# Self attention of the last stage: scores three pieces ahead, slots that begin with turns, and turns as ordinary matmuls with the identity

## The chip, the cores and the metric

The kernel runs on one core of one Trainium2 chip. The metric is device time in microseconds of one execution, and lower is better. TensorE is called PE below, VectorE DVE, ScalarE ACT, GpSimd POOL, and SyncE's DMA queue SP.

## The reference, cut to what matters

The program is a gated stack of two cross attention blocks and two feed forward blocks on 32 sequences of 100 tokens with 128 features. Only the last block, `_L1_ffn_ref`, is touched: self attention with 16 heads of 8 features, layer norm, and a mixture of 8 experts.

```python
def _attention(src, Wq, bq, Wk, bk, Wv, bv, Wo, bo):
    q = (src @ Wq + bq).reshape(B, T, NHEAD, HEAD_DIM)
    k = (src @ Wk + bk).reshape(B, T, NHEAD, HEAD_DIM)
    v = (src @ Wv + bv).reshape(B, T, NHEAD, HEAD_DIM)
    scores = jnp.einsum('bqhd,bkhd->bhqk', q, k) * scale
    probs = jax.nn.softmax(scores, axis=-1)
    out = jnp.einsum('bhqk,bkhd->bqhd', probs, v).reshape(B, T, d)
    return out @ Wo + bo
...
attn_out = _attention(src, Wq, bq, Wk, bk, Wv, bv, Wo, bo)
x = _ln(src + attn_out, ln1_g, ln1_b)
ff = _moe(x, gW, gb, W1, b1, W2, b2)
return _ln(x + ff, ln2_g, ln2_b)
```

## The kernel before

The last stage is `stage_c`. Each engine has its own program, a Python function that writes the instructions in the order in which the engine runs them; engines are ordered against each other by semaphores alone (`wait_ge`, `then_inc`). All data is float32.

The 32 sequences form 8 units of 4 (`UNITS`, `GROUP`; b or u counts them). A sequence's 16 heads are done as two pieces of 8 heads, so there are 64 pieces k (`PIECES`), and the attention part is one loop over k with b, s = divmod(k, 8): s is the slot within the unit. For each piece:

- `scores(k)` on PE: two matmuls of 400 columns into PSUM banks 0 and 1, or 2 and 3, by the parity of k. KBD holds the keys of four heads on a block diagonal, made by `spread` on POOL from FK.
- `subtract(k)` on DVE: the maximum over keys (c_peak), then scores minus maximum into the SBUF tile P.
- `exponent(k)` on ACT: exp in place on P.
- `turn_pieces(k)` on PE: eight transposes of 100x100 (one for each head) from P to PSUM banks 4 and 5.
- `keep(k)` on ACT: a copy of these two banks to the tile PT.
- `weigh(k)` on PE: eight products with VS (values, and a column block of ones that gives the denominators) into bank 6.

After both pieces of sequence m, ACT's `outputs(m)` copies bank 6 to OS, PE's `back(m)` turns OS into bank 7, and DVE's `divide(m)` divides by the denominators and writes U; it counts fu_ready.

Bank 7 is shared by everything else. Around the pieces, each unit has in its slots: `gate(b-2)` and `attended(b+1)` (the output projection of the stage before, 16 matmuls) in s=0; `turn1(b-1)` in s=1; `outer(b-1)` in s=2; `turn0(b+1)` in s=3; `keys(b+1)`, `queries(b+1)`, `values(b+1)` in s=4, 5, 6; `turn2(b-1)` in s=7. Each waits until the reader of bank 7 before it is done: DVE's `enter` (adds and takes the moments of the new unit), `divide`, `residual` or `gate_first`, or a copy on ACT. On ACT, `enter(b+1)` in s=3 and `middle(b-1)` in s=5 are four normalising activations each and stand ahead of `keep(k)`.

The order of the work is written out by hand: the bodies of the loops over k, one for each engine.

Of the kernel before, what the change touches and what calls it, by code (L numbers as in the profile page):

```python
# [20 lines left out]
ACT = mybir.ActivationFunctionType  # L21
# [3 lines left out]
T = 100  # L25
S = 1444
BATCH = 32
GROUP = 4
GROUPS = BATCH // GROUP
TG = GROUP * T  # L30
HEADS, HD = 16, 8
HG = 4
HQ = HEADS * T
# [231 lines left out]
def stage_a(nc, t, x, ctxn, ctxt, x1, h3t):  # L265

    with ExitStack() as ctx:
        def sb(name, shape, dt=F32):
            return ctx.enter_context(nc.sbuf_tensor("a_" + name, shape, dt))
# [17 lines left out]
        CN = sb("CN", [D, 3, KT, D])  # L287
        P = sb("P", [D, 2 * SPAD + 2 * KT * T])
        H = sb("H", [T, 3, GROUP, D])
# [1155 lines left out]
def stage_c(nc, t, x1, att, w1, w2, out):  # L1445

    with ExitStack() as ctx:
        def sb(name, shape, dt=F32):
            return ctx.enter_context(nc.sbuf_tensor("c_" + name, shape, dt))
# [4 lines left out]
        psum, K, tanhs, ident = t.psum, t.K, t.tanhs, t.ident  # L1454
        w, col, row, bank, tok_bank = t.w, t.col, t.row, t.bank, t.tok_bank
        sem = {n: ctx.enter_context(nc.semaphore(n)) for n in C_SIGNALS}
# [12 lines left out]
        FK = sb("FK", [D, 2, TG])  # L1469
        KBD = sb("KBD", [D, 2, GROUP, TG])  # L1470
        VS = sb("VS", [T, 2, GROUP, HEADS, 32])
        P = sb("P", [T, 2, HQ // 2])
        PT = sb("PT", [T, 2, 2, TG])
        OS = sb("OS", [D, TG])
        U = sb("U", [T, 2, GROUP, D])
# [22 lines left out]
        PIECES = UNITS * SLOTS  # L1498
# [99 lines left out]
        def _(act):  # L1598
# [38 lines left out]

            def exponent(k):
                act.wait_ge(sem["sub_ready"], k + 1)
                nc.scalar.activation(P[:, k % 2, :], P[:, k % 2, :], ACT.Exp).then_inc(sem["fe_ready"], 1)  # L1640

            def keep(k):
                act.wait_ge(sem["fpT_psum"], k + 1)
# [49 lines left out]
            queries(0)  # L1693
            values(0)
            exponent(0)
            for k in range(PIECES):
                b, s = divmod(k, SLOTS)
                if s % 2 == 0 and k:
                    outputs(k // 2 - 1)
                if s == 3 and b < LAST:  # L1700
                    enter(b + 1)
                if s == 5 and b:
                    middle(b - 1)
                keep(k)
                if k + 1 < PIECES:
                    exponent(k + 1)
                if s == 1 and b:
                    turned1(b - 1)
                if s == 1 and b >= 2:
                    gate_exponent(b - 2)  # L1710
                if b < LAST:
                    if s == 3:
                        turned0(b + 1)
                    if s == 4:
                        keys(b + 1)
                    if s == 5:
                        queries(b + 1)
                    if s == 6:
                        values(b + 1)
                if s == 7 and b:  # L1720
                    turned2(b - 1)
            outputs(BATCH - 1)
            weights_turned(0)
            for n in range(PIECES):
                u, e = divmod(n, EXPERTS)
# [18 lines left out]
        def _(pe):  # L1744
            mm = nc.tensor.matmul
# [22 lines left out]

            def turn0(u):
                pe.wait_ge(normed[0], u + 1)  # L1770
                if u >= 2:
                    pe.wait_ge(sem["r_used"], u - 1)
                turn(H[:, u % 3], turned[0])
# [17 lines left out]
            def scores(k):  # L1791
                m, c = divmod(k, 2)
                u, j = divmod(m, GROUP)
                pe.wait_ge(sem["kbd_ready"], m + 1)
                pe.wait_ge(sem["fq_ready"], u + 1)
                if k >= 2:
                    pe.wait_ge(sem["sub_ready"], k - 1)
                for b in range(2):
                    r = 2 * c + b
                    dims = slice(32 * r, 32 * r + 32)  # L1800
                    x_ = mm(bank(2 * (k % 2) + b, T, TG), FQ[dims, u % 2, t.ts_(j)], KBD[dims, u % 2, j, :],  # L1801
                            start=True, stop=True, tile_position=(32 * r, 0))
                x_.then_inc(sem["fs_psum"], 1)

            def turn_pieces(k):
                pe.wait_ge(sem["fe_ready"], k + 1)
                if k:
                    pe.wait_ge(sem["fpT_ready"], k)
                for a in range(8):
                    x_ = nc.tensor.transpose(bank(4 + a // 4, T, T, (a % 4) * T), P[:, k % 2, t.ts_(a)], ident[0:T, 0:T])  # L1810
                x_.then_inc(sem["fpT_psum"], 1)

            def weigh(k):
                m, c = divmod(k, 2)
                u, j = divmod(m, GROUP)
                pe.wait_ge(sem["fpT_ready"], k + 1)
                pe.wait_ge(sem["fv_ready"], u + 1)
                if m and not c:
                    pe.wait_ge(sem["os_ready"], m)
                for a in range(8):  # L1820
                    r, q = a % 4, 2 * c + a // 4
                    x_ = mm(psum[32 * r:32 * r + 32, 6, q * T:(q + 1) * T], VS[:, u % 2, j, 8 * c + a, :],  # L1822
                            PT[:, k % 2, a // 4, t.ts_(r)], start=True, stop=True, tile_position=(0, 32 * r), skip_group_check=True)
                x_.then_inc(sem["fo_psum"], 1)
# [40 lines left out]
            def turn2(u):  # L1865
                pe.wait_ge(sem["y_ready"], u + 1)
                if u + 2 < UNITS:
                    pe.wait_ge(sem["fv_ready"], u + 3)
                elif u < LAST:
                    pe.wait_ge(sem["r_used"], u + 1)  # L1870
                else:
                    pe.wait_ge(sem["u_ready"], 2)
                turn(Y[:, u], turned[2])
# [51 lines left out]
            values(0)  # L1925
            scores(0)
            scores(1)
            for k in range(PIECES):
                b, s = divmod(k, SLOTS)
                if k + 2 < PIECES:  # L1930
                    scores(k + 2)
                if s % 2 == 0 and k:
                    back(k // 2 - 1)
                turn_pieces(k)
                if s == 0 and b >= 2:
                    gate(b - 2)
                if b < LAST:
                    if s == 0:
                        attended(b + 1)
                    if s == 3:  # L1940
                        turn0(b + 1)
                    if s == 4:
                        keys(b + 1)
                    if s == 5:
                        queries(b + 1)
                    if s == 6:
                        values(b + 1)
                if b:
                    if s == 1:
                        turn1(b - 1)  # L1950
                    if s == 2:
                        outer(b - 1)
                    if s == 7:
                        turn2(b - 1)
                weigh(k)
            pe.wait_ge(sem["big_loaded"], 32)
            back(BATCH - 1)
            gate(LAST - 1)
# [4 lines left out]
            for n in range(PIECES):  # L1963
                u, e = divmod(n, EXPERTS)
# [17 lines left out]
        def _(dve):  # L1982
            v = nc.vector
# [30 lines left out]
            def subtract(k):  # L2014
                p = k % 2
                dve.wait_ge(sem["fs_psum"], k + 1)
                sc = psum[0:T, 2 * p:2 * p + 2, 0:TG].rearrange("p b (h k) -> p b h k", h=4)
                link(v.tensor_reduce(peak[:, p, :], sc, AX.X, ALU.max))  # L2018
                if k >= 2:
                    dve.wait_ge(sem["fpT_psum"], k - 1)  # L2020
                for b in range(2):
                    last = v.tensor_tensor(P[:, p, b * TG:(b + 1) * TG].rearrange("p (h k) -> p h k", h=4), sc[:, b, :, :],  # L2022
                                           peak[:, p, 4 * b:4 * b + 4].unsqueeze(2).to_broadcast([T, 4, T]), ALU.subtract)
                last.then_inc(sem["sub_ready"], 1)

# [76 lines left out]
            enter(0)  # L2102
            shift(0, 0)
            subtract(0)
            for k in range(PIECES):
                b, s = divmod(k, SLOTS)
                if s % 2 == 0 and k:
                    divide(k // 2 - 1)
                if s == 0 and b >= 2:
                    gate_first(b - 2)  # L2110
                if s == 5 and b:
                    shift(1, b - 1)
                if k + 1 < PIECES:
                    subtract(k + 1)
                if b >= 2:
                    if s == 4:
                        gate_top(b - 2)
                    if s == 6:
                        gate_place(b - 2)
                    if s == 7:  # L2120
                        gate_weights(b - 2)
                if b < LAST:
                    if s == 1:
                        enter(b + 1)
                    if s == 2:
                        shift(0, b + 1)
                if b and s == 3:
                    residual(b - 1)
            divide(BATCH - 1)
            gate_first(LAST - 1)  # L2130
            for n in range(PIECES):
                u, e = divmod(n, EXPERTS)
# [111 lines left out]
```

## Time and profile before

| | |
|---|---|
| median of 3 runs | 2407.45 us (2407.42 to 2408.7) |
| profiled execution, its own time | 2401.97 us |
| its span, first to last instruction | 2400.2 us |
| mean granted clock of PE | 0.917 of 2.4 GHz |
| attention part of the last stage | 1852 to 2156 us |
| PE busy over the span | 2028.5 us, 85% |
| DVE, ACT, POOL busy | 1583.8, 1320.0, 535.9 us |

Busy time is the time in which an engine has an instruction in it. "PEld" is PE's weight load, which overlaps its matmuls, and "PEclk" is the granted clock as a share of 2.4 GHz: 1.00 is the upper of two levels, 0.50 the lower. The profile shows an ordinary f32 matmul as two records and a transpose as one. The timeline's "idle before <-releaser" names who ended a wait; where several semaphores were waited for it names one of them.

### The profile page before, as it was taken

How to read it: one execution, taken by the hardware profiler on the slowest of the kernel's cores; microseconds unless marked ns; L12 is line 12 of the kernel's file. 1: busy time of each engine (PE TensorE's matmuls, PEld its weight loads, DVE VectorE, ACT ScalarE, POOL GpSimd, SP SyncE). 2: the span in 40 equal slices, each digit the busy share in tenths (PEclk: the TensorE clock that was granted, in tenths of full speed). 3: DMA queues.
4: the chain of work that ended last, by engine and by line, in shares of the span. 5: the costliest groups of instructions: out<-in, count | busy, mean ns of one | idle time of the engine just before them, and what ended most of it. 6: DMA issues, size and time to landing. Idle time of an engine off the chain costs nothing. (4 is left out here: it accounts for less than half of the span.)

```text
span 2400.2 us, 45166 instructions
## 1 busy us (share of the span) xinstructions
PE 2028.5 (85%) x17914; PEld 1347.5 (56%) x17914; DVE 1583.8 (66%) x3854; ACT 1320.0 (55%) x2169; POOL 535.9 (22%) x476
## 2 busy tenths in 40 slices
PE   3779997466599999999999999999996888878997
PEld 2546665343355556556565555556564565656776
DVE  5844543787578878877877878878862566654443
ACT  3645554576246666666666666666673555543333
POOL 1410000553302212212222212212212233221111
PEclk9789997666589999999999999999997898879999
DMA  5026662000222313313323323313312110000000
GB/s 160 1 86 187 186 186 75 4 18 17 90 69 104 115 64 113 114 64 117 107 77 108 107 72 113 115 62 115 115 43 94 35 36 18 1 1 4 8 8 11
DMA packets 89104, 181.18 MB, mean 75 GB/s; under 512 B 5907, under 2 KB 63163, under 8 KB 88511
## 3 DMA queue, kind: packets, MB, share of 16 engines
q1 hardware_dynamic: 88894, 178.30, 22.6%
q8 instruction: 143, 2.34, 0.4%
q14 instruction: 67, 0.54, 0.1%
HBM read 95.24 MB, written 11.65 MB: 45 GB/s over the span
## 5 line engine op out<-in xcount | busy, mean ns | idle before, releaser
L1408 DVE TENSOR_REDUCE b_part_max<-psum 128x1 f32<-128x482 f32 (+3 forms) x1248 | 737.3, 650 | 187.6 <-PE psum L1285 173.6
L1198 ACT ACTIVATE b_PT<-psum 128x800 f32<-128x800 f32 x768 | 616.4, 836 | 386.0 <-PE psum L1304 380.0
L1285 PE MATMUL psum<-b_KH,b_QBD 64*128 64x482 f32 (+1 forms) x1152 | 421.4, 443 | 46.3 <-DVE b_part_max L1408 43.4
L1304 PE MATMUL psum<-b_QS,b_KS 64*128 64x200 f32 x3072 | 438.7, 288 | 0.5 <-ACT b_PT L1198 0.3
L1304 PEld LDWEIGHTS psum<-b_QS,b_KS 64*128 64x128 f32 x3072 | 339.6, 186 | 16.2 <-issue 12.1
L1320 PE MATMUL psum<-b_PT,b_V 128*32 128x200 f32 x6144 | 341.1, 339 | 0.6 <-ACT b_PT L1198 0.6
L1285 PEld LDWEIGHTS psum<-b_KH,b_QBD 64*128 64x128 f32 x1152 | 196.6, 188 | 198.0 <-DVE b_part_max L1408 118.6
L1121 POOL TENSOR_TENSOR b_KL<-b_KF,b_KH 128x1444 fp32r<-128x1444 f32 x32 | 106.8, 3337 | 691.9 <-PE psum L1304 669.7
L1320 PEld LDWEIGHTS psum<-b_PT,b_V 128*32 128x32 f32 x6144 | 159.9, 109 | 149.0 <-ACT b_PT L1198 82.3
L2096 DVE SCALAR_TENSOR_TENSOR c_U<-psum,c_gt,c_U 100x128 f32<-100x128 f32 x256 | 72.1, 344 | 129.0 <-PE psum L1917 128.8
L384 POOL TENSOR_TENSOR a_rs<-a_ve,a_half 100x4 f32<-100x4 f32 x48 | 50.0, 1041 | 420.7 <-DVE a_ve L757 420.6
L1917 PE MATMUL psum<-c_W,c_HE 128*100 128x128 f32 x1024 | 123.6, 274 | 14.1 <-ACT c_HE L1682 14.0
L1917 PEld LDWEIGHTS psum<-c_W,c_HE 128*100 128x100 f32 x1024 | 117.2, 167 | 31.8 <-ACT c_HE L1682 18.7
L1272 PE MATMUL psum<-W,b_CT 128*128 128x128 f32 (+1 forms) x768 | 117.7, 293 | 12.7 <-DVE b_part_max L1408 6.7
L804 DVE TENSOR_REDUCE a_peak<-psum 100x1 f32<-100x1446 f32 x32 | 53.2, 1664 | 105.3 <-PE psum L629 105.3
L1272 PEld LDWEIGHTS psum<-W,b_CT 128*128 128x128 f32 (+1 forms) x768 | 92.7, 188 | 41.4 <-DVE b_part_max L1408 37.4
L1682 ACT ACTIVATE c_HE<-psum,C 128x400 f32<-128x400 f32 x128 | 71.9, 587 | 78.9 <-PE psum L1906 75.9
L1646 ACT COPY c_PT<-psum 100x800 f32<-100x800 f32 x64 | 52.5, 821 | 102.0 <-PE psum L1810 102.0
L636 PE MATMUL psum<-a_P,a_CN 128*128 128x100 f32 (+1 forms) x768 | 108.0, 288 | 0.0
L1261 PE MATMUL psum<-b_CT,W 128*128 128x482 f32 (+1 forms) x192 | 101.2, 611 | 5.5 <-DVE b_QF L1382 1.5
L636 PEld LDWEIGHTS psum<-a_P,a_CN 128*128 128x128 f32 (+1 forms) x768 | 95.2, 195 | 18.7 <-issue 11.8
L1535 POOL TENSOR_TENSOR c_rs<-c_ve,c_half 100x4 f32<-100x4 f32 x24 | 24.4, 1015 | 337.0 <-DVE c_ve L1998 337.0
(274 smaller groups left out, 3204.3 us busy)
## 6 DMA issues: line engine op xcount, KB each, us to landing
b_KS<-b_KH SPq DMA_DIRECT2D x64, 722.0 KB
a_CT<-in_ctxt SPq DMA_DIRECT2D x32, 722.0 KB, 4.2
b_CT<-in_ctxt SPq DMA_DIRECT2D x32, 722.0 KB, 4.3
b_KS<-b_KL SPq DMA_DIRECT2D x32, 722.0 KB
a_CN<-in_ctxn SPq DMA_DIRECT2D x32, 704.0 KB
att_scratch<-b_AO SPq DMA_DIRECT2D x32, 200.0 KB, 1.9
c_AIN<-att_scratch SPq DMA_DIRECT2D x8, 800.0 KB
b_MB<-in_mask SPq DMA_DIRECT2D x32, 180.5 KB, 4.4
```

Source lines behind the costliest of these rows:

```text
L636: x_ = mm(bank(7, D, T, TG), CN[0:rows, m % 3, k, :], PTA[0:rows, m % 2, k, :], start=(k == 0), stop=(k == KT - 1))
L1121: pl.tensor_tensor(KL[:, :], KF[:, 0:S], KH[:, j % 2, :].bitcast(F32), ALU.subtract).then_inc(sem["kl_ready"], 1)
L1198: nc.scalar.activation(PT[:, kt % 2, 2 * a:2 * a + 2, :], psum[:, 2 * a:2 * a + 2, 0:TG], ACT.Exp).then_inc(sem["pt_ready"], 1)
L1261: m = mm(bank(b, D, size), w("xkT"), CT[:, j % 2, c:c + size], start=True, stop=True)
L1272: m = mm(bank(b, rows, D, (k % 4) * D), CT[:, j % 2, k * D:k * D + rows], w("xvT"), start=True, stop=True)
L1285: m = mm(bank(b, D, size), QBD[rows, j % 2, tile * D:(tile + 1) * D], KH[rows, j % 2, at_:at_ + size], start=True, stop=True)
L1304: m = mm(bank(p, D, 2 * T, (s % 2) * 2 * T), KS[rows, j % 2, s, kt * D:(kt + 1) * D], QS[rows, j % 2, s * 2 * T:(s + 1) * 2 * T], start=Tr ...
L1320: m = mm(psum[32 * r:32 * r + 32, 6, b * 2 * T:(b + 1) * 2 * T], V[:, j % 2, kt, 4 * b + r, :], PT[:, kt % 2, 2 * b + r // 2, (r % 2) * 2 ...
L1408: v.tensor_reduce(part_max[0:rows, q, c:c + 1], bank(b, rows, CHUNKS[c][1]), AX.X, ALU.max)\
L1682: nc.scalar.activation(HE[:, n % 2, f, :], bank((2 * n + f) % 4, D, TG), ACT.Relu, bias=t.C[:, c:c + 1]).then_inc(sem["moe_h_ready"], 1)
L1917: x_ = mm(bank(4 + n % 2, T, D, j * D), HE[:, n % 2, f, t.ts_(j)], W2[:, c * D:(c + 1) * D], start=(f == 0), stop=(f == 1))
L2096: last = v.scalar_tensor_tensor(out=U3[:, u % 2, j, :], in0=tok_bank(4 + n % 2)[:, j, :], scalar=gt[:, u, 6, j * EXPERTS + e:j * EXPERTS + ...
```

## The change

Four things change, all in the attention part.

1. The scores run three pieces ahead of the piece whose slot it is, not two; P has three buffers, and DVE's `subtract` and ACT's `exponent` run two pieces ahead, not one.
2. A slot on PE begins with `turn_pieces(k)`. Then come `back` and the slot's other steps, then `scores(k + 3)`, and `weigh(k)` last. In slot 5 `weigh(k)` stands ahead of the scores, which there are the first of the next unit.
3. The eight turns of a piece are ordinary matmuls with the identity as the moving operand, not transposes. The other turns (`turn`, `back`) stay transposes.
4. `turn0` and `turn2` get a wait each for a divide (fu_ready).

```diff
@@ tiles
-        P = sb("P", [T, 2, HQ // 2])
+        P = sb("P", [T, 3, HQ // 2])
@@ ACT, exponent and loop
-                nc.scalar.activation(P[:, k % 2, :], P[:, k % 2, :], ACT.Exp).then_inc(sem["fe_ready"], 1)
+                nc.scalar.activation(P[:, k % 3, :], P[:, k % 3, :], ACT.Exp).then_inc(sem["fe_ready"], 1)
             exponent(0)
+            exponent(1)
...
-                if k + 1 < PIECES:
-                    exponent(k + 1)
+                if k + 2 < PIECES:
+                    exponent(k + 2)
@@ PE, turn0, turn_pieces, turn2
+                if u:
+                    pe.wait_ge(sem["fu_ready"], (u - 1) * GROUP + 1)
...
-                    x_ = nc.tensor.transpose(bank(4 + a // 4, T, T, (a % 4) * T), P[:, k % 2, t.ts_(a)], ident[0:T, 0:T])
+                    x_ = mm(bank(4 + a // 4, T, T, (a % 4) * T), P[:, k % 3, t.ts_(a)], ident[0:T, 0:T], start=True, stop=True)
...
                 elif u < LAST:
                     pe.wait_ge(sem["r_used"], u + 1)
+                    pe.wait_ge(sem["fu_ready"], BATCH - 1)
@@ PE, loop
             scores(1)
+            scores(2)
             for k in range(PIECES):
                 b, s = divmod(k, SLOTS)
-                if k + 2 < PIECES:
-                    scores(k + 2)
+                turn_pieces(k)
                 if s % 2 == 0 and k:
                     back(k // 2 - 1)
-                turn_pieces(k)
...
-                weigh(k)
+                if s == 5:
+                    weigh(k)
+                if k + 3 < PIECES:
+                    scores(k + 3)
+                if s != 5:
+                    weigh(k)
@@ DVE, subtract and loop
-                if k >= 2:
-                    dve.wait_ge(sem["fpT_psum"], k - 1)
+                if k >= 3:
+                    dve.wait_ge(sem["fpT_psum"], k - 2)
...
             subtract(0)
+            subtract(1)
...
-                if k + 1 < PIECES:
-                    subtract(k + 1)
+                if k + 2 < PIECES:
+                    subtract(k + 2)
```

On PE, slots 1 and 2 of unit b=1 read before as follows (L1822 is `weigh`, L1801 `scores`, L1810 `turn_pieces`, L1749 `turn1`, L1847 `back`, L1754 `outer`):

```order
L1801 MATMUL psum<-c_KBD,c_FQ 100x400 x2
L1810 MATMUL psum<-K,c_P 100x100 x8
L1749 MATMUL psum<-K,c_U 128x100 x4
L1822 MATMUL psum<-c_PT,c_VS 32x100 x8
L1801 MATMUL psum<-c_KBD,c_FQ 100x400 x2
L1847 MATMUL psum<-K,c_OS 100x128 x4
L1810 MATMUL psum<-K,c_P 100x100 x8
L1754 MATMUL psum<-W,c_OT 100x128 x4
L1822 MATMUL psum<-c_PT,c_VS 32x100 x8
```

After the change the same two slots read (L1813 `turn_pieces`, L1750 `turn1`, L1804 `scores`, L1825 `weigh`, L1850 `back`, L1755 `outer`):

```order
L1813 MATMUL psum<-K,c_P 100x100 x8
L1750 MATMUL psum<-K,c_U 128x100 x4
L1804 MATMUL psum<-c_KBD,c_FQ 100x400 x2
L1825 MATMUL psum<-c_PT,c_VS 32x100 x8
L1813 MATMUL psum<-K,c_P 100x100 x8
L1850 MATMUL psum<-K,c_OS 100x128 x4
L1755 MATMUL psum<-W,c_OT 100x128 x4
L1804 MATMUL psum<-c_KBD,c_FQ 100x400 x2
L1825 MATMUL psum<-c_PT,c_VS 32x100 x8
```

The scores moved from the slot's beginning to between its other steps and `weigh`, and `back` and `outer`, which had the turns between them, now follow each other.

On DVE, from the start of unit b=2, the rows of before are these (L2032 and L2033 `divide`, L2052 to L2056 `gate_first`, L2018 and L2022 `subtract`, L2009 `enter`):

```order
L2032 RECIPROCAL c_inv<-psum 100x16
L2033 TENSOR_TENSOR c_U<-psum,c_inv 100x128
L2052 TENSOR_TENSOR c_gt<-psum,R 100x32
L2055 TENSOR_REDUCE c_sm<-c_gt 100x4
L2056 TENSOR_TENSOR c_gt<-c_gt,c_sm 100x32
L2018 TENSOR_REDUCE c_peak<-psum 100x8
L2022 TENSOR_TENSOR c_P<-psum,c_peak 100x400 x2
L2018 TENSOR_REDUCE c_peak<-psum 100x8
L2022 TENSOR_TENSOR c_P<-psum,c_peak 100x400 x2
L2009 SCALAR_TENSOR_TENSOR c_X<-psum,tanhs,c_XIN 100x512
```

The rows of the changed kernel at that place have the same operations in the same order, with other line numbers. What differs is which pieces they are: the two subtractions ahead of `enter` were those of slots 1 and 2, and are now those of slots 2 and 3.

## Rows read from the trace of the kernel before

**Rows 1.** Busy time by window: the whole part, then its units.

```profile
core 0: us, PE busy (x) PEld busy (x) DVE busy (x) ACT busy (x) POOL busy (x), PEclk, DMA share, GB/s
1852.00:2156.00 304.00, 254.20 (x2416) 173.38 (x2408) 190.29 (x580) 158.13 (x265) 80.14 (x77) 0.86 0.06 18
1857.26:1894.78 37.52, 32.98 (x290) 22.25 (x289) 18.13 (x42) 18.02 (x29) 8.03 (x8) 0.78 0.09 29
1894.78:1931.76 36.98, 31.89 (x312) 22.29 (x313) 22.20 (x58) 21.00 (x35) 11.49 (x11) 0.91 0.09 29
1931.76:1967.95 36.19, 30.56 (x312) 20.79 (x313) 25.04 (x83) 20.43 (x35) 11.50 (x11) 0.95 0.09 30
1931.76:2083.33 151.57, 129.45 (x1248) 88.20 (x1249) 100.23 (x329) 81.96 (x140) 46.00 (x44) 0.90 0.07 22
2083.33:2118.82 35.49, 29.76 (x304) 20.61 (x305) 24.75 (x81) 19.56 (x35) 10.26 (x10) 0.95 0.01 2
2118.82:2153.30 34.48, 25.65 (x236) 17.94 (x240) 20.38 (x65) 16.15 (x25) 3.55 (x3) 0.71 0.01 1
```

**Rows 2.** Waits of PE from 1852 to 2156 us: total, times, longest.

```profile
PE psum L1822 <- ACT c_PT L1646: 19.1, 29, 1.7
PE psum L1801 <- DVE c_P L2022: 10.3, 15, 2.3
PE psum L1749 <- DVE c_U L2041: 5.5, 6, 0.9
PE psum L1801 <- POOL c_KBD L1554: 5.2, 7, 0.7
```

**Rows 3.** Timeline of an even slot, b=2, s=2: start, duration, engine, line.

```profile
1938.54 0.55 PE L1822 MATMUL psum<-c_PT,c_VS 100*32 100x100 f32 x16 [0.57 <-ACT c_PT L1646]
1939.02 0.92 PE L1801 MATMUL psum<-c_KBD,c_FQ 32*100 32x400 f32 x4
...
1940.29 0.64 PE L1847 MATMUL psum<-K,c_OS 128*100 128x128 f32 x4 [0.36 <-ACT c_OS L1652]
1940.66 0.76 PEld L1810 LDWEIGHTS psum<-K,c_P 100*100 100x100 f32 x8
...
1941.26 0.29 DVE L2033 TENSOR_TENSOR c_U<-psum,c_inv 100x128 f32<-100x128 f32 x1
...
1941.66 0.82 ACT L1646 COPY c_PT<-psum 100x800 f32<-100x800 f32 x1 [1.42 <-PE psum L1810]
...
1941.70 1.09 PE L1754 MATMUL psum<-W,c_OT 128*100 128x128 f32 x8
```

**Rows 4.** Timeline of the slots s=3 to 6 of the same unit.

```profile
1943.53 0.98 DVE L2018 TENSOR_REDUCE c_peak<-psum 100x8 f32<-100x800 f32 x1
...
1943.68 0.92 PE L1801 MATMUL psum<-c_KBD,c_FQ 32*100 32x400 f32 x4 [0.41 <-DVE c_P L2022]
...
1944.53 0.69 PEld L1810 LDWEIGHTS psum<-K,c_P 100*100 100x100 f32 x8 [0.59 <-ACT c_P L1640]
...
1944.54 1.05 DVE L2022 TENSOR_TENSOR c_P<-psum,c_peak 100x400 f32<-100x400 f32 x2
...
1946.34 0.54 PE L1749 MATMUL psum<-K,c_H 100*128 100x100 f32 x4 [0.92 <-DVE c_U L2041]
...
1952.92 1.64 ACT L1603 ACTIVATE c_Y<-c_U,c_nb,c_rs 100x128 f32<-100x128 f32 x4
...
1955.17 0.87 ACT L1640 ACTIVATE c_P<-c_P 100x800 f32<-100x800 f32 x1
...
1955.94 0.58 ACT L1628 ACTIVATE c_FQ<-psum,xbq 128x400 f32<-128x400 f32 x1
...
1956.62 0.92 PE L1801 MATMUL psum<-c_KBD,c_FQ 32*100 32x400 f32 x4 [0.75 <-POOL c_KBD L1554]
```

**Rows 5.** Timeline, b=2, s=0 to 1: `gate`, loads of `attended`, DVE's `enter`.

```profile
1930.54 0.84 PE L1754 MATMUL psum<-W,c_YT 128*100 128x8 f32 x8
...
1931.73 3.53 PEld L1766 LDWEIGHTS psum<-W,c_AIN 128*100 128x100 f32 x32 [0.44 <-issue]
...
1935.95 0.74 DVE L2009 SCALAR_TENSOR_TENSOR c_X<-psum,tanhs,c_XIN 100x512 f32<-100x512 f32 x1
```

**Rows 6.** Timeline, weight loads of the turns in b=2, s=4.

```profile
1948.65 1.39 PEld L1810 LDWEIGHTS psum<-K,c_P 100*100 100x100 f32 x8
```

More of the change, by code:

```diff
@@ L2018, in subtract @@
                 link(v.tensor_reduce(peak[:, p, :], sc, AX.X, ALU.max))
-                if k >= 2:
-                    dve.wait_ge(sem["fpT_psum"], k - 1)
+                if k >= 3:
+                    dve.wait_ge(sem["fpT_psum"], k - 2)
                 for b in range(2):
-                    last = v.tensor_tensor(P[:, p, b * TG:(b + 1) * TG].rearrange("p (h k) -> p h k", h=4), sc[:, b, :, :],
+                    last = v.tensor_tensor(P[:, k % 3, b * TG:(b + 1) * TG].rearrange("p (h k) -> p h k", h=4), sc[:, b, :, :],
                                            peak[:, p, 4 * b:4 * b + 4].unsqueeze(2).to_broadcast([T, 4, T]), ALU.subtract)
```

## The prediction

> **What bounds the kernel now.** Read first the windows of the stage [rows 1]. The part that the change touches lasts from 1852 to 2156 us, 304 us of the 2400.2 us span; the rest of the program keeps its instructions, and I count it at no change. TensorE (PE) is busy 254 of these 304 us, VectorE (DVE) 190, ScalarE (ACT) 158: PE is the fullest engine but not full. Its granted clock is 0.86 on average, so with the two levels 1.2 and 2.4 GHz (0.5 and 1) it ran at the lower one for 304 x 0.14 / 0.5 = 85 us. A unit (four sequences, eight slots) takes 37.5 us for b=0, 37.0 for b=1, 151.6 for the four units b=2 to 5, 35.5 for b=6 (up to the gate of the next) and 34.5 for b=7. The fastest whole unit, 36.2 us, is one of those with the highest clock, 0.95.
>
> Then the waits of PE [rows 2]: 19.1 us for the copy of the turned pieces (`keep`, L1646), 10.3 for DVE's subtraction, 5.5 for the residual, 5.2 put down to KBD. Together 40 us, 5 a unit.
>
> The timeline of one even slot [rows 3] tells what the change rearranges. Weights x values (`weigh`) steps in 0.48 us (1938.54 to 1939.02). The scores follow, then `back` at 1940.29 after 0.36 us of waiting for ACT's copy, then the turns, from 1940.66 (eight loads in 0.76 us), then `outer` at 1941.70, which must wait until DVE's divide has read bank 7 (its second half ends 1941.55). From the start of `back` to the start of `outer` is 1.41 us, and `back`'s own loads are done when the turns' begin, after 0.37: **in even slots the turns run for nothing, inside the wait for the divide.** In odd slots [rows 4] they do not: scores at 1943.68, turns at 1944.53 (a step of 0.85), then `turn0`, which waits 0.92 us for DVE's residual.
>
> **The ordinary matmuls.** An ordinary f32 matmul stands in the trace as two records, each with its own weight load: the 16 matmuls of `attended` are 32 loads in 3.53 us, 0.110 each [rows 5]. A turn of now is one record, 0.69 to 0.76 us for eight. Eight ordinary ones are 16 records. Below: the transposes' own pace, 0.69/8 = 0.086, gives 1.38 us; above: `attended`'s 0.110, with 128 columns moving instead of 100, gives 1.77. I take 1.38, since 0.110 x 100/128 is 0.086 as well and the loads have the same 100 columns as the turns. A turn block so grows by 0.69 us; 64 of them add 44 us of PE work at the full clock, 69 at the upper bound. Below nothing it can't cost, as the number of records doubles.
>
> On this the Trainium skill speaks against the change: "Perfetto Trace Analysis", Transposes, asks that logical transposes use the transpose operation and not a standard matmul. The rows agree on the count; by that rule alone the sum would be the 44 us.
>
> **The clock.** Before the fall near 1948.65 PE had run weigh, scores, eight turns, four more transposes, weigh, scores and `back`, with little idle time; the turns after it take 1.39 us of loads for eight instead of 0.69 to 0.76 [rows 6], the lower level. So the clock fell although PE was full, largely of transposes. The turns of the pieces are the largest block of transposes (512 of them), and as they become ordinary matmuls I expect the full clock nearly throughout, except for a short stretch at slot 5, where PE will idle most, in every third unit or so. All that the lower level can cost now is 85 x 0.84 / 2 = 36 us (254 of 304 us busy is 0.84). The Trainium skill, "TensorE: Matmul & The Clock Gate", Part 4, says that transpose mode does not count as PE-busy for the clock; the trace fits that. By the rule alone the change would give back up to those 36 us, against the 44 of the longer turns.
>
> **The new order, slot by slot, at the full clock** (unit b from 2 to 5). Steps: turns 1.38, `back` to next 1.41, scores 0.85, weigh 0.48, DVE's peak and subtraction 2.06, ACT's copy `keep` 0.82, exponent 0.87, FQ and FK 0.58 each, a projection such as `outer` 0.93 of its 1.09 (its tail lies beside the next step), a group of four transposes 0.4 (half of eight), signals between engines about 0.1 each [rows 3, 4]. From the gate's start (1930.54) to that of `attended` (1931.76) is 1.2, `attended` 3.6 [rows 5]. ACT's next instruction starts some 0.1 before the end of the one ahead, as FQ at 1955.94 behind an exponent that ends at 1956.04 [rows 4]. All new slots begin with turns, so the divide's wait behind `back` has no cover any more.
> - s=0: 1.38 + 1.41 + 1.2 + 3.6 + 0.85 + 0.48 = 8.9.
> - s=1: `turn1` needs bank 7 emptied by DVE's `enter`. DVE now does the subtraction of piece s=3 before it, and the scores of s=3 come only after `attended`: 0.95 + 2.06 + 0.75 + 0.1 = 3.85 us after these scores start, while PE gets there after 0.85 + 0.48 + 1.38 = 2.7. A new wait of 1.1. Slot: 1.38 + 1.1 + 0.4 + 0.85 + 0.48 = 4.2.
> - s=2: 1.38 + 1.41 + 0.93 + 0.85 + 0.48 = 5.0.
> - s=3: `turn0` waits for the residual, queued behind a subtraction in the same way: 1.3 instead of 0.9. Slot 4.4.
> - s=4 and 5 together, from the start of slot 4: the divide is done at 2.7, `keys` done at 3.6, scores and weigh to 4.8, turns to 6.2, `queries` to 7.0. ACT: subtraction of s=6 done 4.8, exponent to 5.7, FK to 6.2, the four normalisations `middle` (1.64 us, [rows 4]) to 7.7, `keep` to 8.5. So weigh waits 1.5 us, to 9.0. Exponent to 9.2, FQ to 9.7; the next unit's first scores wait for it 0.75 (as now, where the row names KBD [rows 4]) and end at 10.6.
> - s=6: 5.0 again; s=7: 1.38 + 0.4 + 0.85 + 0.48 = 3.1.
>
> Sum 41.3 us. The gains are in it: no wait for OS, none for `keep` outside slot 5 (the scores now run there), none for the scores' own subtraction. Units b=2 to 5: 4 x 41.3 - 151.6 = +13.6. b=1 has no gate (1.2 less): 40.1 - 37.0 = +3.1. b=6, counted up to the next gate: 40.1 - 35.5 = +4.6. b=0, walked in the same way, begins with the same fill and has fewer steps; it comes to 37.8, +0.3, since the lower clock that it has now (0.78) goes. b=7 has no `attended`, keys, queries or values: 2.1 + 3.1 + 5.0 + 3.0 + 3.1 + 3.5 + 3.0 + 3.0 = 25.8 against 34.5 at a clock of 0.71: -8.7. The first step behind the stage, now at the lower clock, gives perhaps -2. Stretches at the lower clock that stay: +4. Total **+15 us**. The third buffer of P and the added waits for fu_ready cost nothing: the divides that they name ended a slot earlier, and P's third place is used by a subtraction that otherwise waited for the turns; without that cover it would be up to 10.3 us [rows 2].
>
> The sum stands against the profiled execution, 2401.97 us; the median of the runs is 5.5 us more, and I carry that difference: 2407.5 + 15 = 2422.5.
>
> **Rivals.**
> - *PE becomes the pace* (faster). The waits that I give to slots 1, 3, 5 (1.1, 1.3, 1.5, 0.75: 4.7 a unit) are stacked latencies of DVE and ACT, both under 66% busy [rows 1]. If their work of two pieces ahead is done earlier than I put it, they go: 15 - 6 x 4.7 = -13, 2394. For it: subtraction and exponent have a slot more of slack. Against: the order on DVE and ACT puts `enter`, the residual and `middle` behind that very work. It decides once more than 2.5 us a unit are gone. 0.16.
> - *Half of it* (no change): about 2.5 us a unit gone, 2403 to 2412. 0.14.
> - *The clock is not held*: as many stretches as now. The units, 309 us in my walk at the full clock, would grow by the 36 us less what falls into PE's waits, say 25 to 30, instead of 4: 2443 to 2448. For it: the new waits are PE idle time. Against: far fewer transposes. 0.13.
> - *The forecast*, +5 to +30: 0.57.
>
> **How the numbers follow.** A measurement of this kernel tells about 0.2% (4.8 us) from no change. Faster 0.16, same 0.14, slower 0.70 (forecast and third rival). The range leaves out about half of the first rival below and of the third above: 2398 to 2445, which holds the 25 us of the upper bound on the turns too; the forecast's own range is 2412 to 2437.
>
> **What would show it.** In the changed profile: the turns as 1024 records with some 1.4 us a block; mean clock of the stage above 0.95; PE waits for c_PT nearly confined to one place a unit; new waits of `turn1` for c_X and, in every even slot, of gate, outer, keys and values for the divide (c_U), about 0.9 each, some 29 us in all; units of about 41 us, the last one shorter than now. I am wrong if these divide waits are missing, if a turn block takes under 1.2 us, or if the clock stays at 0.86.

## The result, and the profile after

| | before | after |
|---|---|---|
| median | 2408.07 us (4 runs) | 2499.02 us (4 runs, 2487.6 to 2505.4) |
| after / before | | 1.0373, 95% interval 1.0349 to 1.0397 |
| profiled execution, span | 2400.2 us | 2503.6 us |
| stage, from its first scores to its last `weigh` | 302.3 us | 400.9 us |
| granted clock in the stage | 0.87 | 0.76 |

The kernel is 3.7% slower, 91 us; +15 was forecast. Of the 103.4 us between the two profiled spans 98.6 lie in the stage. Executions in the chip's slower state are left out of all ratios; among the kernels below only *weights as moving data* had any, two of six, and its profile (stage, clock and low time in the table) is of one of them.

First the page of the profile after: the granted clock in 40 slices of 62.6 us, in tenths, and the two groups that are the new turns.

```profile
PEclk9789996765599999999999999999977878759999
...
L1813 PE MATMUL psum<-K,c_P 100*100 100x100 f32 x1024 | 140.1, 307 | 0.0
L1813 PEld LDWEIGHTS psum<-K,c_P 100*100 100x100 f32 x1024 | 127.2, 214 | 17.9 <-issue 16.9
```

The 1024 records are there. Their loads take 127.2 us, 1.99 a block, against 1.38 that I had put at the full clock. The digits 77878759 cover the stage. The windows of PE say what that means: the stage, then slots 1 to 5 of unit b=1, then three neighbouring stretches of the unit before.

```profile
core 0: us, PE busy (x) PEld busy (x) DVE busy (x) ACT busy (x) POOL busy (x), PEclk, DMA share, GB/s
1855.55:2256.44 400.89, 350.95 (x2925) 259.31 (x2924) 191.21 (x578) 159.75 (x264) 80.54 (x78) 0.76 0.04 14
1921.32:1945.62 24.30, 19.34 (x212) 13.26 (x208) 14.91 (x43) 14.20 (x25) 6.39 (x7) 1.00 0.13 43
1900.00:1904.00 4.00, 4.00 (x28) 2.48 (x28) 2.17 (x4) 1.34 (x2) 0.00 (x0) 0.50 0.02 4
1904.00:1908.00 4.00, 4.00 (x28) 3.15 (x20) 1.56 (x3) 0.75 (x2) 0.00 (x0) 0.50 0.00 0
1908.00:1912.00 4.00, 4.00 (x34) 2.98 (x31) 0.00 (x0) 1.33 (x3) 0.00 (x0) 0.50 0.00 0
```

Two things are to be seen. Where the clock is 1.00, slots 1 to 5 take 24.30 us. And PE stays at the lower level for 12 us although it is busy in all of them. Before, the stage was at the lower level for 0.13/0.5 of 302 us, some 79; after, for 0.24/0.5 of 401, some 192. DVE and ACT do what they did (191.2 and 159.8 us, [rows 1]).

What changed is not how often the clock falls. The granted clock of the profile of before has 13 stretches at the lower level in the stage, 6.2 us on average and at most 13.7; after has 11, 17.5 on average and at most 58.0. A fall of before (at 1948.7, the one that the prediction discusses), then one of after (at 1881.1) and the low stretch that it begins, in windows:

```profile
1943.68:1948.65 4.97, 3.98 (x40) 2.28 (x41) 3.90 (x14) 4.54 (x9) 0.85 (x1) 1.00 0.00 0
```

```profile
1876.00:1881.00 5.00, 2.81 (x35) 1.78 (x34) 2.13 (x5) 4.70 (x9) 0.00 (x0) 1.00 0.01 3
1881.10:1918.50 37.40, 35.09 (x200) 25.27 (x199) 11.58 (x21) 10.70 (x15) 6.97 (x7) 0.50 0.00 0
```

Ahead of both falls PE had waited, 0.99 of 4.97 us and 2.19 of 5.00, and so it had ahead of every other fall in the two stages. Once low, the clock stayed low for 37.5 us in the second case, although PE was busy for 35.09 us of the 37.40 in the window.

The timeline of PE at the end of one low stretch and in the full one behind it. L1813 is `turn_pieces`, L1825 `weigh`, L1804 `scores`, L1767 `attended`.

```profile
1903.39 0.90 PE L1825 MATMUL psum<-c_PT,c_VS 100*32 100x100 f32 x16
1904.22 2.99 PE L1813 MATMUL psum<-K,c_P 100*100 100x100 f32 x16
1907.14 1.66 PE L1804 MATMUL psum<-c_KBD,c_FQ 32*100 32x400 f32 x4
...
1909.56 2.99 PE L1813 MATMUL psum<-K,c_P 100*100 100x100 f32 x16
1912.34 1.06 PE L1850 MATMUL psum<-K,c_OS 128*100 128x128 f32 x4
1914.17 5.90 PE L1767 MATMUL psum<-W,c_AIN 128*100 128x128 f32 x32 [0.77 <-DVE c_U L2041]
1919.99 0.92 PE L1804 MATMUL psum<-c_KBD,c_FQ 32*100 32x400 f32 x4
...
1923.84 0.53 PE L1750 MATMUL psum<-K,c_U 100*128 100x100 f32 x4 [0.86 <-DVE c_X L2017]
...
1925.63 1.66 PE L1813 MATMUL psum<-K,c_P 100*100 100x100 f32 x16
1927.12 0.60 PE L1850 MATMUL psum<-K,c_OS 128*100 128x128 f32 x4
1928.49 1.09 PE L1755 MATMUL psum<-W,c_OT 128*100 128x128 f32 x8 [0.77 <-DVE c_U L2041]
```

The same block of turns takes 2.99 us in the low stretch and 1.66 in the full one. The low stretch ends inside `attended` (near 1918.6), a run of 32 records with nothing between them.

Waits of PE from 1852 to 2260 us (total, times, longest):

```profile
PE psum L1755 <- DVE c_U L2041: 16.1, 21, 0.8
PE psum L1825 <- ACT c_PT L1646: 7.5, 8, 1.0
PE psum L1782 <- DVE c_U L2041: 5.4, 7, 0.8
PE psum L1750 <- DVE c_X L2017: 5.2, 6, 0.9
PE psum L1750 <- DVE c_U L2049: 4.8, 6, 0.8
PE psum L1804 <- POOL c_KBD L1554: 4.5, 6, 0.7
```

Against [rows 2], the wait of `weigh` for ACT's copy fell from 19.1 to 7.5 us and that of the scores for DVE's subtraction from 10.3 us to a single one of 2.3, at the start of the stage. In their place stand 21.5 us of waits for the divide (L1755 `gate`, `outer` and `values`, L1782 `keys`) and 5.2 for `enter`. These six rows sum to 43.5 us, the four of [rows 2] to 40.1: the waits moved and do not account for 98 us. So the open question is why the clock stays low.

### The profile page after: what moved, and what is told of

Its sections match the earlier page's. It is cut to its first block and busy times, and to the rows that moved or that the text cites. A ratio compares the mean times of both kernels' runs of the same rounds, so it can differ in the third digit from the quotient of the medians.

```text
span 2503.6 us, 46190 instructions
## 1 busy us (share of the span) xinstructions
PE 2128.7 (85%) x18426; PEld 1436.2 (57%) x18426; DVE 1585.5 (63%) x3854; ACT 1321.6 (53%) x2169; POOL 535.6 (21%) x476
## 5 line engine op out<-in xcount | busy, mean ns | idle before, releaser
L1813 PE MATMUL psum<-K,c_P 100*100 100x100 f32 x1024 | 140.1, 307 | 0.0
L1813 PEld LDWEIGHTS psum<-K,c_P 100*100 100x100 f32 x1024 | 127.2, 214 | 17.9 <-issue 16.9
L1272 PEld LDWEIGHTS psum<-W,b_CT 128*128 128x128 f32 (+1 forms) x768 | 92.7, 188 | 41.4 <-DVE b_part_max L1408 37.5
```

The lines of the kernel that those rows point to most:

```text
L1272: m = mm(bank(b, rows, D, (k % 4) * D), CT[:, j % 2, k * D:k * D + rows], w("xvT"), start=True, stop=True)
L1813: x_ = mm(bank(4 + a // 4, T, T, (a % 4) * T), P[:, k % 3, t.ts_(a)], ident[0:T, 0:T], start=True, stop=True)
```

## The experiments

Durations of the stage, its clock and its busy time come from one window of one profile, first scores to last `weigh`. Each ratio is against the kernel before in the same series of runs: medians 2408.0 us in the first set, 2410.7 in the second, 2409.1 in the third. "Low" is the time at the lower level, length x (1 - clock) / 0.5.

| kernel | / before, 95% interval | stage, us | clock | low, us |
|---|---|---|---|---|
| before | 1 | 302 | 0.87 | 79 |
| after | 1.0349 to 1.0397 | 401 | 0.76 | 192 |
| new order, turns as transposes | 1.0319 to 1.0443 | 395 | 0.61 | 308 |
| old order, turns as matmuls | 1.0018 to 1.0041 | 311 | 0.96 | 25 |
| after, weights as moving data | 1.0216 to 1.0267 | 411 | 0.74 | 214 |
| after, 16 transposes | 1.0284 to 1.0412 | 391 | 0.78 | 172 |
| after, scores behind `back` | 1.0180 to 1.0252 | 364 | 0.79 | 153 |
| the same, scores of full height | 1.0086 to 1.0134 | 330 | 0.98 | 13 |
| after, filler behind `back` | 1.0090 to 1.0172 | 339 | 0.94 | 41 |
| after, `back` ahead of the turns | 1.0060 to 1.0134 | 324 | 0.94 | 39 |
| old order, three ahead, transposes | 1.0032 to 1.0085 | 317 | 0.82 | 114 |
| before, even turns as matmuls | 1.0033 to 1.0065 | 313 | 0.89 | 69 |
| before, filler in odd slots | 0.9986 to 1.0015 | 299 | 0.92 | 48 |
| old order, matmuls, odd scores late | 1.0010 to 1.0036 | 306 | 0.96 | 24 |

### First set: data, kind of turn, or order

In the texts on record of this set the letters name the theories. D says that the clock counts little for data that is mostly zero, as the identity; I says that the new order pulls it down.

**The new order with transposes**: the order's share.

```diff
-    x_ = mm(bank(4 + a // 4, T, T, (a % 4) * T), P[:, k % 3, t.ts_(a)], ident[0:T, 0:T], start=True, stop=True)
+    x_ = nc.tensor.transpose(bank(4 + a // 4, T, T, (a % 4) * T), P[:, k % 3, t.ts_(a)], ident[0:T, 0:T])
```

> The new order, the third buffer and the new waits, with the turns as transposes again (the eight turns of a piece are one record each). Theory I (the new idle stretches of PE behind the divide and at slots 1, 3, 5 pull the clock down): they are all still there and even longer, the clock of the stage stays near 0.76, and the time is 2440 us or more.

Measured: median 2501.8 us, in theory I's range; the clock is 0.61, the lowest of all and lower than either theory said. Its stage in the windows:

```profile
1850.59:2245.51 394.92, 348.86 (x2413) 230.10 (x2412) 191.69 (x578) 163.02 (x264) 80.69 (x78) 0.61 0.05 14
```

PE has 512 records fewer than after (x2413 against x2925) and is busy as long, since nearly all of it runs at half speed. The order, together with three ahead and the added waits, brings the whole loss without the ordinary matmuls.

**The old order with matmuls**, the other half of the change: the opposite edit, in the kernel before.

> The kernel before with one edit, the turns of the pieces as ordinary matmuls with the identity. At the full clock this adds 0.8 us in odd slots and 0.6 in even ones, 45 us in all. Theory D: the clock falls more often and stays low longer, as in the changed kernel; another 20 to 35 us; 2470 to 2490. Theory I: PE idles less than before, so the clock is no lower than before (0.86 in the stage): 2440 to 2455.

Measured: 2414.3 us, clock 0.96. Both theories missed, by 25 us and more. Its stage:

```profile
1851.01:2161.95 310.94, 274.21 (x2925) 203.91 (x2924) 189.83 (x578) 158.04 (x264) 80.75 (x78) 0.96 0.06 18
```

The timeline of its PE in an even slot:

```profile
1942.63 0.65 PE L1847 MATMUL psum<-K,c_OS 128*100 128x128 f32 x4 [0.35 <-ACT c_OS L1652]
1943.11 1.58 PE L1810 MATMUL psum<-K,c_P 100*100 100x100 f32 x16
1944.53 1.04 PE L1754 MATMUL psum<-W,c_OT 128*100 128x128 f32 x8
```

From `back` to `outer` it is 1.90 us instead of 1.41 [rows 3]: of the 0.7 us by which the turns grew, a third lies in the wait for the divide. PE is busy 20 us more than before, not 44, as the rest of its work runs faster; the stage is 9 us longer. The identity matmuls hold the clock, in this order.

**Weights as moving data**: the turns multiply by a block of a weight tile, so PT is no longer P turned, and all that follows from it is other data.

```diff
-    ... P[:, k % 3, t.ts_(a)], ident[0:T, 0:T], start=True, stop=True)
+    ... P[:, k % 3, t.ts_(a)], t.W[0:T, 0:T], start=True, stop=True)
```

> The changed kernel with one operand replaced: the turns multiply by a 100x100 block of dense weights instead of the identity. Same instructions, shapes, addresses' sizes, waits; the turned scores are then no softmax weights, so the result isn't the reference's. Theory D: with dense data the clock stays at the upper level nearly throughout, as the prediction's walk assumed: stage clock above 0.93, time 2425 to 2440. Theory I: nothing changes in the idle stretches: clock 0.76, 2490 to 2505.

Measured: the four executions of its ratio took 2466.1 to 2497.7 us, their clock over the whole kernel 0.897 to 0.912, against 2487.6 to 2505.4 us and 0.894 to 0.902 of after. D asked for 2425 to 2440 and falls: dense data doesn't bring the clock back. The ratio still lies below that of after, 1.0241 against 1.0373, some 32 us, with intervals apart. The spread of the four is as large as that, so whether the data has a small share stays open; theory I's range, 2490 to 2505, was missed as well.

**Sixteen transposes for eight matmuls**, each turn done twice, so that the number of records is that of after.

```diff
-    for a in range(8):
-        x_ = mm(...)
+    for a in (*range(8), *range(8)):
+        x_ = nc.tensor.transpose(...)
```

> The changed kernel with each piece's eight turns as transposes, done twice over (16 records, as the ordinary matmuls have). It separates the kind of the turn from its length. Theory D, and identity matmuls count as little as transposes: the same as the changed kernel, 2485 to 2510, stage clock 0.74 to 0.78. If ordinary matmuls with the identity count for something and transposes for nothing: lower clock and over 2515. Theory I: also 2490 to 2505, so this run alone does not tell D from I.

Measured: 2498.9 us against 2499.0, clock 0.78 against 0.76. A transpose so seems to count for the clock like a matmul record: against the new order with eight transposes the only edit is eight more for each piece, and the clock is 0.78 instead of 0.61 at no more time (2501.8 us there). Its timeline shows more, at the end of a low stretch:

```profile
1884.99 0.90 PE L1825 MATMUL psum<-c_PT,c_VS 100*32 100x100 f32 x16
1885.82 2.90 PE L1813 MATMUL psum<-K,c_P 100*100 100x100 f32 x16
1888.52 0.73 PE L1850 MATMUL psum<-K,c_OS 128*100 128x128 f32 x4
```

The windows there:

```profile
1885.30:1888.80 3.50, 3.50 (x34) 3.20 (x27) 0.00 (x0) 0.53 (x2) 0.00 (x0) 0.50 0.00 0
1888.80:1892.20 3.40, 2.63 (x27) 1.09 (x25) 2.85 (x6) 1.10 (x2) 0.00 (x0) 1.00 0.00 0
```

The clock rises at 1888.80, and for nearly 3 us ahead of that (from 1885.82) PE had done transposes and nothing else.

### Second set: what in the order

In the old order PE does `back`, turns and projection in one dense run. In the new one the divide's 0.77 us of idle time stands between `back` and the projection, and scores and `weigh` follow each other. Theory R is that this run, once broken, no longer raises the clock; the rival is that three ahead does it by itself.

**Scores behind `back`**: in even slots the scores fill the idle time.

```diff
     back(k // 2 - 1)
+    if k + 3 < PIECES:
+        scores(k + 3)
...
-if k + 3 < PIECES:
+if k + 3 < PIECES and (s % 2 or not k):
     scores(k + 3)
```

> The changed kernel; in even slots the scores of three pieces ahead stand directly behind back, in PE's wait for the divide, instead of ahead of weigh. Ordinary matmuls as turns. Theory R (the lower clock comes from the new order: PE idles for the divide between back and the projection, and scores and weigh stand side by side; no unbroken stretch of dense matmuls is left that would raise the clock again). Two forms of it: R-idle, the idle time is what counts: it is filled here, so the stage's clock comes above 0.93 and with 0.8 us saved in each even slot the time is 2400 to 2415 us. R-scores, the scores and weigh products hold the clock down as idle time does: they stand in the middle of the stretch now, the clock stays at 0.75 to 0.8 and the time is over 2460 us.

**Filler behind `back`**: four matmuls that nothing reads, in the same place.

```diff
     back(k // 2 - 1)
+    for f in range(4):
+        mm(psum[0:T, 6, 400:500], w("fo")[:, 0:T], w("fk")[:, 0:T], start=True, stop=True)
```

> The changed kernel with work added: behind each back four matmuls of two weight blocks into columns of PSUM bank 6 that nobody reads, some 0.7 us at the full clock, in the time in which PE waits for the divide. Both forms of R: back, filler and projection follow the turns without a break; the clock of the stage comes above 0.93 and the kernel gets faster by doing more, 2420 to 2445 us. If the clock has another cause: 2495 us or more.

**`back` ahead of the turns**, as before the change; all else as after.

```diff
-    turn_pieces(k)
     if s % 2 == 0 and k:
         back(k // 2 - 1)
+    turn_pieces(k)
```

> The changed kernel with back ahead of the turns in even slots, as in the kernel before; the scores stay between the projection and weigh. PE now idles ahead of back (0.7 us, for ACT's copy OS) and not behind it. Both forms of R: back, turns and projection are one stretch again: stage clock above 0.93, 2415 to 2440 us. If slots in which weigh is followed by no scores, or scores by weigh, are the cause by themselves: clock below 0.85 and over 2460 us.

**Three ahead alone**: after with transposes, in the order of before (scores, `back`, turns; in slot 5 the scores behind `weigh`).

> The kernel before (transposes, scores at the slot's beginning, then back, turns, projection, weigh) with only the distance changed: scores three pieces ahead, subtraction and exponent two ahead, third buffer of P; in slot 5 the scores stand behind weigh. R: the stretch is intact, the clock is that of before (0.85 to 0.9), and the waits for the subtraction (10.3 us) are gone: 2395 to 2410 us. If running three ahead is itself what pulls the clock down, over 2440 us.

Measured: 2462.8, 2442.6, 2432.4 and 2421.8 us. The first three lie where theory R had them (the first by its form R-scores), the fourth in neither range. First the filler's timeline at a gate and its stage:

```profile
1948.32 0.60 PE L1850 MATMUL psum<-K,c_OS 128*100 128x128 f32 x4
1948.75 0.87 PE L1939 MATMUL psum<-W 128*100 128x100 f32 x8
1949.68 0.84 PE L1755 MATMUL psum<-W,c_YT 128*100 128x8 f32 x8
```

```profile
1860.42:2199.80 339.38, 307.10 (x3173) 236.91 (x3172) 191.30 (x578) 158.70 (x264) 80.63 (x78) 0.94 0.05 17
```

The stage with `back` ahead of the turns:

```profile
1860.70:2184.85 324.15, 280.45 (x2925) 211.73 (x2924) 193.95 (x578) 159.05 (x264) 80.75 (x78) 0.94 0.05 17
```

Its PE waits ahead of `back` for ACT's copy OS, 16.9 us, where after waits 21.5 for the divide behind it (waits from 1856 to 2200 us):

```profile
PE psum L1850 <- ACT c_OS L1652: 16.9, 24, 1.7
```

The timeline and the stage with the scores behind `back`:

```profile
1918.83 0.60 PE L1850 MATMUL psum<-K,c_OS 128*100 128x128 f32 x4
1919.36 0.92 PE L1804 MATMUL psum<-c_KBD,c_FQ 32*100 32x400 f32 x4
1920.21 0.94 PE L1782 MATMUL psum<-c_HT,W 128*128 128x400 f32 x2
```

```profile
1852.12:2216.48 364.36, 335.06 (x2925) 244.67 (x2924) 189.99 (x578) 159.63 (x264) 80.59 (x78) 0.79 0.05 15
```

The filler adds 248 records, all of them needless, and takes 56 us away from after. `back` moved by one place takes 67 away, mostly not by shorter waits: PE is idle for 43.7 us of its stage, 49.9 after. The scores fill the same idle time as the filler and the clock stays at 0.79. They take 36 us away, of which some 21 are idle time gone (PE is idle for 29.3 us of the stage, 49.9 after); the rest is an estimated 17 us of clock, for 153 us low instead of 192. Three ahead alone was expected to gain and does not: it is 0.3 to 0.9% slower at clock 0.82, so some of what is left of the loss lies there. The two large waits of PE before (19.1 and 10.3 us, [rows 2]) stand where they did, a little longer (waits from 1852 to 2175 us):

```profile
PE psum L1825 <- ACT c_PT L1646: 22.7, 29, 1.5
PE psum L1804 <- DVE c_P L2029: 11.9, 16, 2.3
```

### Third set: why scores are no filler, and the old order

The scores use 32 rows of the array a matmul (the 32x400 of their rows), the two of a piece side by side. **Full height**: the kernel with the scores behind `back`, each score matmul of every slot over all 128 rows, one after the other. The scores are then other numbers.

```diff
-x_ = mm(..., FQ[dims, u % 2, t.ts_(j)], KBD[dims, u % 2, j, :],
-        start=True, stop=True, tile_position=(32 * r, 0))
+x_ = mm(..., FQ[:, u % 2, t.ts_(j)], KBD[:, u % 2, j, :],
+        start=True, stop=True)
```

> The kernel with the scores in the gap behind back, and its scores made from all 128 rows of FQ and KBD at once instead of 32 rows each in two row groups side by side: as many instructions and columns, but one after the other, 1.4 us a piece instead of 0.85 at the full clock (35 us more in all), and scores that sum over four times as many rows, so the result isn't the reference's. R-scores (the row-tiled scores weigh as little as idle time for the clock): more work raises the clock to above 0.93 in the stage, and the time is 2425 to 2445, below the 2463 of the kernel that it is made from. If the scores have no part in it: the clock stays near 0.8 and the 35 us come on top, 2490 to 2510.

Measured: 2437.2 us, 26 less than its partner, though each scores step takes longer. Its timeline and its stage:

```profile
1922.45 0.60 PE L1850 MATMUL psum<-K,c_OS 128*100 128x128 f32 x4
1922.89 1.51 PE L1804 MATMUL psum<-c_KBD,c_FQ 128*100 128x400 f32 x4
1924.23 0.83 PE L1782 MATMUL psum<-c_HT,W 128*128 128x400 f32 x2
```

```profile
1856.39:2186.22 329.83, 301.86 (x2925) 225.38 (x2924) 189.98 (x578) 159.85 (x264) 80.89 (x78) 0.98 0.05 17
```

Scores to the next step is 1.34 us here and 0.85 there, at the full clock in both, and the stage is still 35 us shorter. PE is busy for 92% of the stage in both, at clock 0.79 and 0.98. So in this order 32-row scores do far less for the clock than full-height ones. How far that is the rows of the array, and how far the longer time that the same matmuls take, is not told apart; and since the edit reaches the scores of all slots, it doesn't show that the place behind `back` is the one that counts.

**Even turns as matmuls** in the kernel before (`if k % 2 == 0:` matmul, else transpose), where they lie in the divide's wait:

> The kernel before with ordinary matmuls as turns in even slots alone, where the transposes lie hidden in the wait for the divide. Cost at the full clock 0.6 us in 32 slots, 19 us; gain: the time at the lower clock falls from 82 us to 20 to 40, worth 20 to 25 us. Theory R: 2395 to 2410. If it needs the longer turns in all slots to hold the clock: 2420.

**Filler in odd slots** of the kernel before, three matmuls as above ahead of `weigh`:

> The kernel before with work added that nobody reads: three matmuls of two weight blocks into free columns of bank 6 ahead of weigh in odd slots, 0.5 us at the full clock, where PE waits 0.57 us and more for the copy of the turned pieces in three of four odd slots. Theory R: the clock is held longer at almost no cost, 2395 to 2407 us. If short idle times don't matter for the clock: 2412 to 2420, since slot 3 has no such wait to hide it in.

**Odd scores late**: the old order with matmuls, and in odd slots `scores(k + 2)` just ahead of `weigh`:

> The kernel before with ordinary matmuls as turns in all slots, and in odd slots the scores (two pieces ahead as before) between the projection and weigh, where they cover the wait for the copy of the turned pieces. At the full clock it saves 0.5 us in odd slots against 2414 us of the matmul turns alone: 2400 us. Theory R-scores warns: scores, weigh, scores then stand side by side at each change from odd to even slot, 2.2 us of work that weighs little, and the clock falls more often than in that kernel (21 us in the stage): then 2410 to 2430.

Measured: 2420.9, 2409.3 and 2414.8 us; before, on the same chip, 2409.1. The stages of the first two:

```profile
1851.48:2164.74 313.26, 269.68 (x2669) 195.72 (x2668) 192.30 (x578) 156.74 (x264) 80.78 (x78) 0.89 0.06 18
```

```profile
1859.34:2158.55 299.21, 257.15 (x2605) 183.48 (x2604) 190.06 (x578) 158.69 (x264) 80.80 (x78) 0.92 0.06 18
```

The first has fewer records than the old order with all turns as matmuls (x2669 against x2925) and is no faster, as its clock is 0.89 and not 0.96: theory R's 2395 to 2410 was a miss, and the 2420 set against it came true. The second raises the clock to 0.92 in its profile and is no faster, 2 us above theory R's range and 3 below the other. The third equals its partner: late scores by themselves harm nothing while `back`, turns and projection stay together, but the 14 us that were hoped for did not come. None of the twelve beats the kernel before.

## Why the prediction was wrong

The direction was forecast (0.70 for slower), the size was not: 2499.0 lies 54 us above the range. That it is slower at all was no luck, as the terms at the full clock hold; the largest part of the 91 us came from a term that was put at nearly nothing. By its own steps:

- **The ordinary matmuls: right in size.** A turn block's step at the full clock is 1.49 us (1925.63 to 1927.12), and 1.42 in the old order with matmuls (1943.11 to 1944.53); 1.38 was put.
- **The walk at the full clock: right.** Slots 1 to 5 of b=1 took 24.30 us; 4.2 + 5.0 + 4.4 + 10.6 = 24.2 were put. The divide waits are there, 0.77 each instead of about 0.9 and 21.5 us instead of 29, `turn1` waits 0.86 for c_X where 1.1 was put, and `weigh` waits for c_PT 8 times, 7.5 us. The gain of 8.7 us for the last unit did not come: from its gate to the last `weigh` it took 42.8 us (2213.67 to 2256.44) instead of 34.5, at clock 0.54. So neither *PE becomes the pace* nor *half of it* came true: the latencies stack as the walk had them.
- **The clock: the step that failed.** "As they become ordinary matmuls I expect the full clock nearly throughout", with +4 us for what stays low. It stayed low for some 192 us. At the stage's busy share of 0.875 that costs an estimated 192 x 0.875 / 2 = 84 us. The stage took 401 us; the walk's 309 with the 6 us that the stage of before has beyond its units [rows 1] is 315, 86 less. That one term is nearly the whole error.
- **Its reason was wrong too.** I had read the fall of [rows 6] as coming of transposes with PE full. PE was not full: from 1943.68 to the fall at 1948.7 it was busy for 3.98 of 4.97 us, with the wait of 0.92 us that [rows 4] show in it. Nor did transposes as such hold the clock down: sixteen of them give the clock of the 16 matmul records, going from eight to sixteen raised it from 0.61 to 0.78, and a stretch of transposes alone was followed by a rise. So the rule of the Trainium skill ("TensorE: Matmul & The Clock Gate", Part 4), that transpose mode does not count as busy, is not borne out by this kernel's runs. The one on Transposes ("Perfetto Trace Analysis") is, but weakly: in the old order the matmuls cost 0.18 to 0.41%, 6 to 7 us and not 44, because the divide's wait hides a third of it in even slots and the higher clock pays for much of the rest.
- **The rival *the clock is not held* was right in kind and had the wrong bound.** Its "as many stretches as now" came true (11 against 13), but it took their length in the kernel before, 85 us together, as the most that could be low, and the cost of all of them as 36 us. Nothing in the profile supports such a bound: the stage could lie at the lower level for all of its length. With the turns as transposes in the new order it did for 308 of 395 us.
- **What keeps it down.** Shown: the order does it (with transposes the whole loss), the kind of turn at the same count of records does not, and the data at most in small part. Dense work between `back` and the projection, or `back` ahead of the turns again, brings the clock to 0.94 and 56 to 67 us back. So where PE waits counts more than how long: with `back` ahead of the turns PE is idle for 43.7 us instead of 49.9. Shown too: with 32-row scores behind `back` the clock is 0.79, with full-height scores in all slots 0.98. The falls themselves come behind waits, before and after; in the new order the clock then takes longer to return, though PE is busy for nearly all of that time. Busy time in the windows does not tell scores and `weigh` from dense work.
- **What stays open.** Why three ahead alone lowers the clock to 0.82, and why even turns as matmuls give 0.89 for more work, is not settled: both shift the times at which low stretches begin, and one profile of each doesn't separate chance places from causes. That `weigh` (32 columns of the array) counts as little as the scores is argued from its place beside them, and was not tried.

## What to carry to other kernels

Where a stage shows two clock levels, look at an order's dense runs first: a reorder that left the sum of the waits alike cost 3.7% here, with the turns as transposes too, and moving one step by one place gave 67 of 91 us back. What the clock can cost is bounded by the busy time that the stage would have at the full clock, once over (an estimated 267 us after the change, 350.95 - 84), not by the time that it is low now. Look ahead of each fall for waits, as [rows 4] show them, before the kind of work is blamed. A step that hides in a wait, as the turns did behind `back`, may also be what keeps the clock, so count that before it is moved out.

## What was not expected of the hardware

- PE stayed at the lower level while it was busy without a break (12 of 12 us from 1900 to 1912, granted 0.50), in a mix of a projection's end, 32-row scores, 32-column `weigh` and turns.
- Work that nobody reads made the kernel faster: 248 more records, 2442.6 instead of 2499.0 us; and scores at 1.34 us a step instead of 0.85 gave 2437.2 instead of 2462.8.
- Transposes and ordinary matmul records of the same count gave the same time (medians 2498.9 and 2499.0 us) and nearly the same clock (0.78 and 0.76). Sixteen transposes a piece took no longer than eight (2498.9 and 2501.8 us), with the clock at 0.78 instead of 0.61.
